# Expert tiles: one engine loop over the turns, in place of nine turns written out

## The reference, cut to what matters

```python
probs = jax.nn.sigmoid(logits)                      # 8 experts: 4 of width 256, 4 of width 512
topw, sel = jax.lax.top_k(probs, 2)
topw = topw / (topw.sum(-1, keepdims=True) + 1e-20)
combine = jnp.sum(topw[:, :, None] * onehot, axis=1)
h = jnp.square(jax.nn.relu(jnp.einsum('td,edw->tew', xf, W1e)))
y = jnp.einsum('tew,ewd->ted', h, W2e)
out = jnp.einsum('ted,te->td', y, combine)
```

## Time and profile before

| | before |
|---|---|
| median of 3 runs | 779.54 us (778.46 to 780.48) |
| the profiled execution | 778.08 us |
| its span, first to last instruction | 776.3 us |
| TensorE busy | 629.6 us (81%) |
| VectorE / ScalarE / POOL busy | 470.6 / 309.2 / 336.5 us |
| instructions on TensorE | 4950 matmuls and 4950 weight loads |
| instruction queues | q8: 46 packets, 0.75 MB; q14: 45 packets, 0.37 MB |

### The profile page before, as it was taken

The page is one execution under the profiler, slowest core; times in us unless marked ns, Lnnn a source line. Parts: engine busy times, 40 slices in busy tenths (PEclk is TensorE's granted clock), DMA queues, the critical chain, the costliest instruction groups (busy, mean ns, idle before and its releaser), DMA issues. The chain is left out here.

```text
span 776.3 us, 16107 instructions
## 1 busy us (share of the span) xinstructions
PE 629.6 (81%) x4950; PEld 545.7 (70%) x4950; DVE 470.6 (61%) x1218; ACT 309.2 (40%) x666; POOL 336.5 (43%) x312
## 2 busy tenths in 40 slices
PE   0179487999999999999999997307998998978873
PEld 0179366787777878878788775206997887878873
DVE  0157476687879778797887873636453454545441
ACT  3123025334453443535335354005553544455442
POOL 6733223230824608155271735142353443455474
PEclk9779789999999999999999999656998999999897
DMA  7470686010111102111020101332353444466563
GB/s 231 132 198 1 136 246 209 2 55 2 56 55 50 62 1 75 34 54 55 21 88 0 54 28 55 108 110 69 63 92 54 79 70 71 78 100 103 86 112 49
DMA packets 38621, 61.07 MB, mean 79 GB/s; under 512 B 6282, under 2 KB 31890, under 8 KB 37906
## 3 DMA queue, kind: packets, MB, share of 16 engines
q1 hardware_dynamic: 23266, 36.80, 16.2%
q0 software_dynamic: 14976, 22.10, 15.3%
q10 hardware_dynamic: 288, 1.05, 0.4%
HBM read 30.54 MB, written 28.34 MB: 76 GB/s over the span
## 5 line engine op out<-in xcount | busy, mean ns | idle before, releaser
L1440 POOL DMA_INDIRECT out<-y,token_at x72 | 113.1, 1571 | 128.9 <-SPq L1420 128.0
L701 POOL DMA_INDIRECT queue_d<-row,slot x64 | 64.1, 1002 | 164.0 <-DVE slot L1013 146.9
L1519 DVE SCALAR_TENSOR_TENSOR act_w<-relu,queue_rows 128x512 f32<-128x512 f32 (+1 forms) x72 | 45.6, 633 | 118.0 <-ACT relu L1464 97.7
L1177 PE MATMUL bank<-xt_hi,w_first 128*128 128x512 f32 x256 | 94.1, 413 | 0.9 <-DVE second_half L891 0.9
L1177 PE MATMUL bank<-w_first,xt_hi 128*128 128x512 f32 x256 | 84.0, 410 | 2.5 <-DVE xt_lo L881 1.5
L693 POOL TENSOR_TENSOR second_half<-second_half,q_inv 128x512 f32<-128x512 f32 x64 | 64.9, 1041 | 42.4 <-DVE q_inv L900 42.3
L751 ACT ACTIVATE second_half<-second_half 128x512 f32<-128x512 f32 x64 | 40.3, 631 | 88.0 <-DVE second_half L891 87.8
L759 ACT ACTIVATE k_exps<-bank,k_negmax 128x512 f32<-128x512 f32 x64 | 44.2, 691 | 75.1 <-DVE k_negmax L907 74.9
L1561 PE MATMUL bank<-w_hi,a_hi 128*128 x224 | 70.4, 314 | 0.4 <-DVE a_lo L1525 0.3
L1464 ACT ACTIVATE relu<-bank 128x512 f32<-128x512 f32 (+1 forms) x72 | 36.2, 503 | 77.3 <-PE bank L1561 77.3
L1561 PE MATMUL bank<-w_lo,a_hi 128*128 x224 | 63.8, 285 | 0.0
(11 more groups left out here) (174 smaller groups left out, 1570.6 us busy)
## 6 DMA issues: line engine op xcount, KB each, us to landing
queue_rows<-queue_d SPq DMA_DIRECT2D x74, 129.0 KB, 2.1
store<-in_L_ffn_w SPq DMA_DIRECT2D x4, 1536.0 KB, 9.2
out<-res SPq DMA_DIRECT2D x8, 512.0 KB, 2.9
h_d<-store SPq DMA_DIRECT2D x7, 512.0 KB, 8.9
h_in<-h_d SPq DMA_DIRECT2D x7, 512.0 KB, 3.9
wqk<-in_L_attn_w_qkv SPq DMA_DIRECT2D x1, 2048.0 KB, 8.0
queue_d<-filler SPq DMA_DIRECT2D x1, 1290.0 KB, 11.5
out<-y,token_at POOLq DMA_INDIRECT x72, 4.0
```

The source lines that it names most:

```text
L701: pool.indirect_dma_start(out=queue_d, in_=row[:, t, c, :], in_offset=None, out_offset=bass.IndirectOffsetOnAxis(ap=slot[:, TT * c + t:TT ...
L1177: last = nc.tensor.matmul(o, a, c, start=(n == 1), stop=(n == 3 * len(pairs)))
L1440: pool.indirect_dma_start(out=out, in_=y[:, j % RING, :], in_offset=None, compute_op=ALU.add, out_offset=bass.IndirectOffsetOnAxis(ap=toke ...
L1519: nc.vector.scalar_tensor_tensor(out=act_w[:, u % 2, 0:width], in0=relu[:, u % 2, 0:width], scalar=rows[:, u, DIM:DIM + 1], in1=relu[:, u ...
```

## The change

The first turn stays straight code. The other eight become one engine loop, `Fori(1, 9)`, on each of the three engines; its body holds the two copies of a turn once. Inside it the turn's number is a register, so the waits' values, the row of the table and the semaphore counts are worked out in registers. Each pass loads two words, the previous turn's and its own, since the steps of slots 0 and 1 run `down` for the last two tiles of the previous turn; expert numbers are shifted out of them where they are used. Which copy runs is now told by the expert of tile 8 x turn - 2 (slot 6 of the previous word), not of tile 8 x turn. For these inputs both tell the same. After the loop the last word is loaded once more.

```diff
     def need(engine, s, value):
-        if value > 0:
+        if not isinstance(value, int) or value > 0:
             engine.wait_ge(s, value)
 
     def all_turns(engine, step):
-        words = []
-        for turn in range(TILES // SLOTS):
-            words.append(engine.value_load(table.word_of[0:1, turn:turn + 1], min_val=0, max_val=EXPERTS ** SLOTS - 1))
-            with engine.If((words[turn] & (EXPERTS - 1)) < WIDE):
+        def word(turn):
+            return engine.value_load(table.word_of[0:1, bass.ds(turn, 1)], min_val=0, max_val=EXPERTS ** SLOTS - 1)
+
+        def of_turn(turn, words):
+            first = words[0] >> (3 * (SLOTS - AHEAD)) if len(words) > 1 else words[0]
+
+            with engine.If((first & (EXPERTS - 1)) < WIDE):
                 for u in range(SLOTS):
                     step(words, turn, u, MAXW)
             with engine.Else():
                 for u in range(SLOTS):
                     step(words, turn, u, NARROW_W)
-        return words
+
+        of_turn(0, [word(0)])
+        with engine.Fori(1, TILES // SLOTS) as i:
+            of_turn(i, [word(i - 1), word(i)])
...
             def take_token(turn, u):
-                need(dve, added[u % RING], adds_before(turn - 1, u + RING) * 16)
+                if not isinstance(turn, int):
+                    dve.wait_ge(added[u % RING], adds_before(turn - 1, u + RING) * 16)
...
-            def expert_at(words, j):
+            def expert_at(word, u):
 
-                return (words[j // SLOTS] >> (3 * (j % SLOTS))) & (EXPERTS - 1)
+                return (word >> (3 * u)) & (EXPERTS - 1)
 
             def step(words, turn, u, width):
                 j = turn * SLOTS + u
-                e[u] = expert_at(words, j)
-                up(j, u, e[u], width)
+                up(j, u, expert_at(words[-1], u), width)
                 x_turn(j + AHEAD, u, (u + AHEAD) % SLOTS, turn + (u + AHEAD) // SLOTS)
...
-                if j >= 2:
-                    down(j - 2, u, e[u - 2] if u >= 2 else expert_at(words, j - 2), width)
+                if not isinstance(j, int) or j >= 2:
+                    down(j - 2, u, expert_at(words[-1], u - 2) if u >= 2 else expert_at(words[0], SLOTS + u - 2), width)
...
-            words = all_turns(pe, step)
+            all_turns(pe, step)
             act_turn(TILES - 1, 1, MAXW)
+            last = pe.value_load(table.word_of[0:1, TILES // SLOTS - 1:TILES // SLOTS], min_val=0,
+                                 max_val=EXPERTS ** SLOTS - 1)
             for u in range(2):
-                down(TILES - 2 + u, u, expert_at(words, TILES - 2 + u), MAXW)
+                down(TILES - 2 + u, u, expert_at(last, SLOTS - 2 + u), MAXW)
```

More of the change, by code:

```diff
@@ L1481, in step @@
                 x_high(j + AHEAD, u)
-                if j >= 1:
+                if not isinstance(j, int) or j >= 1:
                     act_high(j - 1, u + 1, width)
-                if j >= 2:
+                if not isinstance(j, int) or j >= 2:
                     take_y(turn, u - 2)
@@ L1589, in down @@
                     for f in range(chunks)], 3 * chunks).then_inc(down_done, 1)
-            def expert_at(words, j):
-                return (words[j // SLOTS] >> (3 * (j % SLOTS))) & (EXPERTS - 1)
+            def expert_at(word, u):
+                return (word >> (3 * u)) & (EXPERTS - 1)
             def step(words, turn, u, width):
                 j = turn * SLOTS + u
-                e[u] = expert_at(words, j)
-                up(j, u, e[u], width)
+                up(j, u, expert_at(words[-1], u), width)
                 x_turn(j + AHEAD, u, (u + AHEAD) % SLOTS, turn + (u + AHEAD) // SLOTS)
-                if j >= 1:
+                if not isinstance(j, int) or j >= 1:
                     act_turn(j - 1, u + 1, width)
-                if j == 2:
+                if isinstance(j, int) and j == 2:
                     pe.wait_ge(w2_lo_ready, 2)
                     pe.wait_ge(pads_zero, 2)
-                if j >= 2:
-                    down(j - 2, u, e[u - 2] if u >= 2 else expert_at(words, j - 2), width)
-            e = {}
+                if not isinstance(j, int) or j >= 2:
+                    down(j - 2, u, expert_at(words[-1], u - 2) if u >= 2 else expert_at(words[0], SLOTS + u - 2), width)
             x_turn(0, 0, 0, 0)
```

## The result

| | kernel before | changed kernel |
|---|---|---|
| median of the runs, us | 779.0 (775.57 to 780.48) | 770.33 (769.65 to 771.4) |
| ratio of the two, 95% interval | | 0.9885 (0.9857 to 0.9914) |
| profiled execution, us (span) | 778.08 (776.3) | 770.90 (769.1) |
| first product of turn 0, then of turn 5, us | 529.95, 681.33 | 530.46, 678.70 |
| adds of tiles 38 and 71 start, us | 685.09, 768.55 | 682.75, 761.18 |

The changed kernel is 8.7 us faster; 4.3 to 4.5 were forecast. In the profiled pair it is 7.2 us of span, and the stages give: first part +0.5, wide turns (turn 0's first product to turn 5's) 151.38 to 148.24, so -3.1; the narrow turns' adds, tile 38 to 71, 83.46 to 78.43, **-5.0**; +0.5 in the two pieces between and behind.

A forecast was written before the change was run, and what follows sets the result against it. TensorE was taken to bound the wide turns, SP's program and the adds the narrow ones. Savings of 3.6 + 0.7 = 4.3 us gave 775.2 on the median's scale, forecast as 775.0 us; own range 771 to 777, widened to 769.0 to 779.5.

The forecast's parts named there:

- rival D: Wide turns: turn 1's exit lands in loaded code and the clock holds; 5.7 us less, 769.3 us; chance 0.06.
- Code is used again: TensorE's loop: one slow exit jump of 3.7 us after turn 1, every later jump 0.24 to 0.3 us, nothing fetched again.
- rival A: TensorE's looped code isn't kept, so each turn has two slow jumps; 820 us; chance 0.10.
- The gaps of the wide turns: TensorE's gaps at wide turn ends: 4.2 us into turn 2, 0.8 into turns 3 and 4, 1.05 into turn 5.
- rival B: Wide turns: four small gaps of 0.8 to 1.05 us lower TensorE's clock, each costing 2.3 us; 783 us; chance 0.05.
- The clock after turn 2's gap: Wide turns: TensorE's lowered clock after the 4.2 us gap into turn 2 costs 2.3 us.
- What that saves: Wide turns: losses of 10.1 us against 13.7, so 3.6 us saved, arriving in full at the first narrow add.
- The narrow turns: Turns after the wide ones: three TensorE gaps shrink to about 2.0 us, covered by finished y; 0.7 us saved, bounds 0 and 3.3.
- still 83 us: Sign in the profile after: the stretch from the first narrow add to the last stays at 83 us.
- Rival E: Narrow turns: TensorE's gaps count after all, three times some 4.6 us more for gap and clock; 761 us; chance 0.03.
- ScalarE and VectorE at 0: Turn ends of ScalarE and VectorE grow by some 1.3 us but are not on the path, so they cost 0.

The follow-up runs named there:

- the second profile: Kernel before, unedited, profiled again: wide turns 146.55 us, adds 38 to 71 86.4 us; the changed kernel, likewise repeated: 148.38 and 77.9 us, median 771.06, ratio 0.9882.

## Why the prediction was right, and where it was wrong

The forecast, 775.0 us, was 4.7 us too high. The time lies inside the range of 769.0 to 779.5, 1.3 us above its lower end, but 0.7 us below the forecast's own range of 771 to 777: only the margin for rival D takes it in, and what D stood for (turn 1's exit into loaded code) did not happen. That it lies inside is luck. The half of the sum on the wide turns and the code was right in its mechanism; the half on the narrow turns, where most of the gain arose, was wrong.

*Code is used again*: right. One slow jump, forecast 3.7 us, measured 3.698; all later ones forecast 0.24 to 0.3, measured 0.07 to 0.25; q8 silent from turn 3 on. That refutes rival A. (The attention loop that this step leaned on is larger than its 1,227 instructions: the trace records 782 products, 782 weight loads and 78 rows of the sequencer in a pass, 1,642. The step holds the better for it.) The rule behind A, that an engine's instruction memory holds two pages in order and a taken branch out of them waits for a fetch (the Trainium skill, "Runtime: NRT & Kernel Launch", Instruction fetch mechanics), does not hold for TensorE here: seven branches back over 932 instructions, with a jump across half of them in each pass, took 0.21 to 0.25 us and fetched nothing. The larger memory that the same section gives TensorE agrees with it.

*The gaps of the wide turns*: right in size. Forecast 0.8, 0.8 and 1.05 us at the heads of turns 3, 4 and 5, measured 0.81, 0.79 and 0.94, and 4.2 for turn 2, measured 4.43; small gaps left the clock at 1.00. That refutes rival B, whose price has a slip besides: 775 + 9 is 784, not 783. The clock after turn 2's gap, forecast 2.3 us, cost 1.9: tiles 15 and 16 took 13.18 us (582.98 to 596.16), 6.28 over two of 3.45, less the gap. From tile 15 to turn 5's first product the changed kernel took 95.7 us (582.98 to 678.70), 9.5 over 25 tiles of 3.45, against a forecast of 4.2 + 2.3 + 0.8 + 0.8 + 1.05 = 9.15.

*What that saves*: forecast 3.6, measured 3.1 in this pair of profiles, but 1.8 *lost* in the second. The first narrow add came 2.3 us earlier, 2.8 counted from turn 0, where 3 to 4 were forecast. The step took the kernel before at one profile's word. Its 13.7 us of loss hold 3 us of clock behind the gap into turn 2, and that comes and goes: of the kernels with this head written out, the clock stayed up after 2.67 us and, in the run with turns 5 to 8 in the loop, after 2.89, and fell after 2.73, 2.87 and 2.97. The looped kernels always have a gap over 4 us there, and always paid (clock 0.50 to 0.76 in the 6 us behind it). On the mean of the two pairs the wide turns gave 0.7 us, which the medians do not bear out: with turns 5 to 8 alone in the loop the ratio is 0.9936, with the whole change 0.9885, a difference of 0.5% or 4.0 us. That kernel's gap at turn 5 is 1.05 us longer than the kernel before's (4.39, 3.34), so about 3 us are the wide turns' by this estimate, with an uncertainty of nearly 3.

*The narrow turns*: **this step failed.** "The cover is the backlog, so I give nothing for TensorE [...] Bounds 0 and 3.3; I take 0.7", and "still 83 us" from the first narrow add to the last. Measured: 78.4, so 5.0 us in this pair and 8.5 in the second. The new gap was right (2.0 forecast, 2.17 to 2.19 measured); that it is covered was wrong. The bound of 3.3 us came from SP's waits on y, summed over the stretch, and the rows on the backlog show it where it was large: y of 707.52 and 709.35, in the middle of a turn. The view that answers the question is the distance from the end of a y to the start of its own add, tile by tile. The kernel before at tiles 54 and 62, behind the heads of turns 7 and 8, ScalarE's y and then the add:

```profile
725.31 0.39 ACT L1476 ACTIVATE y<-bank 128x256 f32<-128x256 f32 x1 [0.89 <-PE bank L1561]
727.28 1.64 POOL L1440 DMA_INDIRECT out<-y,token_at  x1 [0.52 <-SPq L1420]
...
747.55 0.39 ACT L1476 ACTIVATE y<-bank 128x256 f32<-128x256 f32 x1 [0.89 <-PE bank L1561]
749.13 1.63 POOL L1440 DMA_INDIRECT out<-y,token_at  x1 [0.56 <-SPq L1420]
```

From the end of y to the add 1.58 and 1.19 us; 1.14 is the least that any narrow tile shows, that is an add that starts as soon as its y allows. The backlog was used up, or nearly, at these heads; at the head of turn 6 (tile 46) 2.11 us were left. In the second profile it was used up at all three, 1.20 us each. In the changed kernel the tiles of the first view:

```profile
717.62 0.39 ACT L1482 ACTIVATE y<-bank 128x256 f32<-128x256 f32 x1 [0.21 <-PE bank L1568]
721.84 1.56 POOL L1446 DMA_INDIRECT out<-y,token_at  x1 [0.52 <-SPq L1426]
...
736.96 0.40 ACT L1482 ACTIVATE y<-bank 128x256 f32<-128x256 f32 x1
741.63 1.56 POOL L1446 DMA_INDIRECT out<-y,token_at  x1 [0.52 <-SPq L1426]
```

3.83 and 4.27 us, and 1.95 at tile 46: a gap of 2.2 is covered, with 0.8 us to spare at the tightest head. A larger backlog cannot form, since y has a ring of four: between 684 and 760 us ScalarE's y waited 14 times (12.1 us) for an add to free a buffer, in the kernel before twice. With the gaps of the kernel before nothing is left, and beyond that each us counts: from 6.5 us of gaps to 14.4, 6.8 more in the adds, and from 14.4 to 20.4 (6.0 more), 6.0. TensorE and the adds take turns at being the bound, and neither view that sums the waits of the stretch tells it: a late landing at a change of expert and a late y behind a head can stand in for each other.

*Rival E*, "the narrow gaps count after all", was the true mechanism and had 0.03. Its price, 3 x 4.6 = 13.8 us on top of the rest, was about twice too high. It took the clock's fall as saved at all three heads; measured over 6 us from each head, the clock was 0.74, 0.52 and 0.72 before and 0.72, 1.00 and 0.72 after, so it was saved at turn 7 alone. That head, before and after:

```profile
721.50:727.50 6.00, 6.00 (x29) 6.00 (x30) 1.77 (x7) 2.37 (x7) 4.47 (x4) 0.52 0.69 113
...
715.38:721.38 6.00, 6.00 (x49) 5.72 (x50) 2.96 (x11) 3.58 (x11) 4.66 (x3) 1.00 0.58 90
```

By an estimate that is some 2.8 us for the clock (the differences of these shares, times 6 us) beside 6.9 for the gaps, 9.7 us for TensorE. Only 5.0 arrived: once the gaps were covered again, the adds and SP's own work set the pace.

*ScalarE and VectorE at 0*: right, shown by the two runs with one side looped each.

## What to carry to other kernels

A gap of one engine is covered only if the backlog at the end of it is still there: follow the time from one engine's result to its use, item by item, and take its smallest value in each period, not the sum of the waits and not the state in the middle of the period. Then test the cover by lengthening the gap on purpose; here seven idle loads told in one run that the slack was gone. And price a loss by more than one profile if it holds a clock that may or may not fall: the piece that I could price best was the one that did not repeat. Here a loop paid on TensorE because its turns skip long unused copies; changing between loop and written-out code cost one more slow jump, and relieving the second bound (SP's words) brought 4 us with the loop and nothing without it.

## What was not expected of the hardware

- TensorE's clock after a gap of one size goes either way: at 1.00 for the 6 us after gaps of 2.67 and 2.89 us, at 0.50 after 2.97 and after 2.87; and after the changed kernel's narrow heads, 2.17 to 2.19 us, down at two and up at one.
- SP's load of one word from on-chip memory took 0.27 us in the median in the changed kernel (0.59 at most), and 0.28 to 0.32 in the median and up to 0.69 us beside one more transfer per tile, on the path of every narrow tile.
- An add that had a code packet of TensorE beside it late in its course landed 0.6 us or more later than the others (4.3 to 5.2 us after its start against 3.4 to 3.7).
- The time at which turn 0 begins moved between 528.35 and 533.71 us in fourteen profiles, in kernels whose first part is the same but for one operation; a stage's time leaves this scatter out.
